# Respacing VectorE's maxima, norms, gates and shifts in the common order of an attention kernel's heads

## The reference

```
q, k, v = x @ Wq, x @ Wk, x @ Wv          # 16 heads of 64
q, k = rmsnorm(q) * wq, rmsnorm(k) * wk
gate = softplus((k . u_n) / 8)            # per key
bias = -max(i - j, 0) * omega_eff * gate[j], -inf above the diagonal
attn = softmax(q @ k.T / 8 + bias);  y = attn @ v
x = layernorm(x + y @ Wproj)
x = layernorm(x + ffn(x))                 # ternary weights, silu * linear, gelu, gelu, linear
```

## Time and profile before

| | us |
|---|---|
| median of 3 runs (3759.3 to 3764.21) | 3760.38 |
| the profiled execution, its own time | 3759.36 |
| its span, first to last instruction | 3757.6 |
| PE busy (matmuls) | 3330.4 |
| VectorE busy | 1934.7 |
| ScalarE busy | 1872.5 |
| GpSimd busy | 1503.4 |
| first and last matmul L835 of the scores | 177.0, 2530.1 |

### The profile page before, as it was taken

One profiled execution on the slowest core, in us unless ns is written; L12 is line 12 of the kernel. 1 busy time (PEld: TensorE's weight loads), 2 busy tenths in 40 slices (PEclk: granted clock), 3 DMA queues, 4 the chain that ended last, 5 costly groups with the idle time before them and its releaser, 6 DMA issues. The chain is left out here.

```text
span 3757.6 us, 46242 instructions
## 1 busy us (share of the span) xinstructions
PE 3330.4 (89%) x16112; PEld 2546.0 (68%) x16112; DVE 1934.7 (51%) x4076; ACT 1872.5 (50%) x3185; POOL 1503.4 (40%) x1304
## 2 busy tenths in 40 slices
PE   2598898898998988989889889896999999899999
PEld 1476675675666766757667667565788877688887
DVE  4566657657657566576565665734322222133232
ACT  0166666666666666666666666673232222232222
POOL 1265565556655655556556555561111111000000
PEclk9999999999999999999999999997999999999999
DMA  1001111011111110111111101105232222221120
GB/s 48 20 24 39 29 32 38 23 32 40 25 42 44 32 37 24 32 39 26 36 28 32 38 24 32 36 24 157 85 99 87 82 84 88 74 96 39 63 68 18
DMA packets 138776, 179.90 MB, mean 48 GB/s; under 512 B 37808, under 2 KB 70192, under 8 KB 138544
## 3 DMA queue, kind: packets, MB, share of 16 engines
q1 hardware_dynamic: 138544, 176.94, 17.1%
HBM read 83.81 MB, written 42.47 MB: 34 GB/s over the span
## 5 line engine op out<-in xcount | busy, mean ns | idle before, releaser
L333 POOL TENSOR_TENSOR e_lo<-e_all,e_hi 128x512 fp32r<-128x512 f32 (+1 forms) x832 | 1042.0, 1257 | 952.7 <-ACT e_all L546 811.9
L546 ACT ACTIVATE e_all<-ps_s,bias 128x512 f32<-128x512 f32 (+3 forms) x1280 | 782.5, 620 | 191.4 <-PE ps_s L838 130.4
L539 ACT ACTIVATE e_hi<-ps_s,bias 128x512 fp32r<-128x512 f32 (+1 forms) x832 | 558.9, 672 | 311.2 <-PE ps_s L836 197.7
L725 DVE TENSOR_REDUCE maxes<-ps_m 128x1 f32<-128x512 f32 x768 | 525.3, 686 | 365.0 <-PE ps_m L811 360.4
L811 PE MATMUL ps_m<-k_ext,q_max 128*128 128x512 f32 (+3 forms) x1280 | 484.9, 392 | 68.2 <-DVE maxes L725 37.8
L835 PE MATMUL ps_s<-q_twice,k_split 128*128 128x512 f32 (+3 forms) x1280 | 492.7, 385 | 0.0
L836 PE MATMUL ps_s<-q_ext,k_ext 128*128 128x512 f32 (+3 forms) x1280 | 479.6, 375 | 0.0
L869 PE MATMUL ps_v<-e_lo,v_main 128*66 128x512 f32 (+1 forms) x832 | 441.0, 530 | 15.7 <-POOL e_lo L333 15.7
L811 PEld LDWEIGHTS ps_m<-k_ext,q_max 128*128 128x128 f32 x1280 | 249.2, 195 | 215.1 <-DVE maxes L725 70.5
L722 DVE CUSTOM_DVE_ANT_0 ps_m<-ps_m,mask_row 128x128 f32<-128x128 f32 (+3 forms) x512 | 252.6, 493 | 247.9 <-PE ps_m L811 244.2
L860 PE MATMUL ps_v<-e_hi,v_rest 128*66 128x512 f32 (+1 forms) x832 | 330.8, 398 | 0.0
(11 more groups left out here) (198 smaller groups left out, 6469.0 us busy)
## 6 DMA issues: line engine op xcount, KB each, us to landing
q_twice<-q_max SPq DMA_DIRECT2D x256, 128.0 KB, 2.3
yt<-y_out SPq DMA_DIRECT2D x128, 130.0 KB
k_split<-k_ext SPq DMA_DIRECT2D x128, 128.0 KB, 2.2
y_in<-yt SPq DMA_DIRECT2D x128, 128.0 KB, 3.1
r_in<-recip_sums SPq DMA_DIRECT2D x128, 128.0 KB, 3.2
hidden<-gelu SPq DMA_DIRECT2D x64, 256.0 KB, 2.0
a_in<-hidden SPq DMA_DIRECT2D x8, 2048.0 KB, 10.9
x_rows<-in_L_attn_x_dram SPq DMA_DIRECT2D x16, 256.0 KB, 3.0
```

Source lines behind the costliest of these rows:

```text
L333: on.tensor_tensor(e_lo[:, i % LO_RING, off:QB], e_all[:, u_ % E_RING, off:QB], e_hi[:, i % HI_RING, off:QB].bitcast(F32), ALU.subtract).t ...
L539: nc.scalar.activation(e_hi[:, i % HI_RING, off:QB], ps_s[u_ % 2][:, off:QB], ACT.Exp, bias=by).then_inc(hi_done, 1)
L546: nc.scalar.activation(e_all[:, u_ % E_RING, off:QB], ps_s[u_ % 2][:, off:QB], ACT.Exp, bias=by).then_inc(ex_done, 1)
L725: nc.vector.tensor_reduce(maxes[:, qt, kc:kc + 1], ps_m[m % 2][:, 0:width], AX.X, ALU.max).then_inc(mx_free, 1)
```

## The change

It gives other due times to some steps. In pair p, with t0 = 2p: "gate a" at t0 - 0.805, "gate exp" at t0 - 0.78, the norms from t0 - 0.80 in steps of 0.035, the parts of "gate b" from t0 - 0.73 in steps of 0.025, the even head's maxima up to t0 + 0.46, the odd head's from t0 + 0.47 to t0 + 1.17, and each shift 0.08 behind the last maximum of its block. No instruction is added or left out, and none computes anything else.

```
-        at(t0 - 0.78, "gate a", p)
-        at(t0 - 0.75, "gate exp", p)
+        at(t0 - 0.805, "gate a", p)
+        at(t0 - 0.78, "gate exp", p)
         for i in range(8):
-            at(t0 - 0.77 + 0.025 * i, "norm", p, i)
+            at(t0 - 0.80 + 0.035 * i, "norm", p, i)
         for i in range(GATE_PARTS):
-            at(t0 - 0.72 + 0.02 * i, "gate b", p, i)
+            at(t0 - 0.73 + 0.025 * i, "gate b", p, i)
...
-            start, end = (turns[1] + 0.03, t0 + 0.28) if s == 0 else (t0 + 0.29, t0 + 1.29)
+            start, end = (turns[1] + 0.03, t0 + 0.46) if s == 0 else (t0 + 0.47, t0 + 1.17)
             for v, (qt, kc) in enumerate(MAXES):
                 qb = qt // TQ
                 when = max(start + (end - start) * v / (NM - 1), turns[2 * qb + 1] + 0.03)
                 at(when, "max", n, v)
                 if v + 1 == maxes_to(qb):
                     at(when + 0.001, "most", n, qb)
-                    at(when + 0.03, "shift", n, qb)
+                    at(when + 0.08, "shift", n, qb)
```

## The result

The changed kernel takes 3774.16 us (median of 7 runs, 3769.09 to 3776.96) against 3760.26 (7 runs, 3756.68 to 3764.21): ratio 1.0034, 95% interval 1.0022 to 1.0046. It is slower by 14 us, where 3743 us, 17 us faster, had been forecast.

The account below looks back on a forecast made before the run. TensorE was taken as the bound, each pair being a 29.8 us VectorE chain plus 120.3 us of TensorE. Terms of -1.0 us a pair, times 15, and -2 once gave 3743 us; range 3717 to 3777.

Parts of the forecast that it names:

- The failed step: In the VectorE chain, the earlier gate Exp holds TensorE and GpSimd some 5 us; TensorE's 10 us to spare make it free.
- the five maxima: They leave the VectorE chain, about -2.9 us of VectorE work, and cost TensorE 1.15 us in the part it bounds.
- Shift 2 behind turn 5: Even head's shift lands right behind an odd head's turn in the same slot: 1.65 us of TensorE waiting.
- First scores of an even head: Their q_twice copies are issued behind shift 1 and come late: +0.35 us a pair, bounds 0 and 1.
- Shift 3's row: Even head's last shift comes close to the scores needing its row: +0.2 us a pair, bounds 0 and 0.5.
- The clock: TensorE's half-speed stretches, about 1.7 us each: one behind shift 0 goes, one behind shift 2 comes; bounds -1.7 and +1.7.
- Before all scores: Once, ahead of attention's first scores, five maxima leave; the q_twice copies then end the wait: -1.5 us.
- The last pair: Final two heads of attention: half of the -1.5 us way back, giving -2 together with the start.
- C: VectorE chain: GpSimd and VectorE exclude each other throughout, all cover comes back, chain 29.7 us, 3785 us; chance 0.09.
- D: Even head: shift 3's row comes too late, a new wait of 0.5 us plus low clock, 3775 us; chance 0.14.
- B: VectorE chain: GpSimd fills half the place of the five maxima, chain only -1.5 us, 3761 us; chance 0.20.
- the signs of being wrong: Chain 29 us or more, gap above 1 us before even heads' scores, odd-head maxima waiting for VectorE, or new low clock.

Follow-up runs that it names:

- Shifts 0.085: The changed kernel with the shifts 0.085 behind their last maximum instead of 0.08: 3767.3 us, ratio 1.0023 to the kernel before.
- values late: Changed kernel with gate Exp at t0 - 0.75, even head's maxima ending at t0 + 0.28, and its GpSimd value copies and splits due later: 3705.2 us.

## Why the prediction was wrong

**The view of the kernel held.** A pair is one VectorE chain and one TensorE part: in all twelve profiles TensorE's first turn follows the end of the last gate link within 0.1 us.

**The failed step** is this one, on what the early Exp holds up: TensorE and GpSimd "stand still meanwhile", "PE has 10 us to spare in this stretch, so that costs nothing". I saw the hold and sized it (5 us; 5.59 measured). I asked whether TensorE had time to spare before its own next wait, and not what else waits for TensorE in that stretch. The emptying does, and it stands in the very queue that bounds. It made VectorE wait 2.4 us a pair, and the chain is 28.95 us where I had forecast 26.9. With the Exp back it is 27.07, and the time is 33 us lower. The mechanism of the five maxima was right in sign and size. I did expect a stretch at low clock in this part of the chain, and called it covered; it falls on the work that the emptying waits for.

**The other terms.** From the turn to the next root the sum was 1.8 us more; measured 1.26. Shift 2 behind turn 5: 1.65 taken, 1.64 measured. First scores of an even head: 0.35 taken, 0.5 measured, for which the profile names no releaser. Shift 3's row: 0.2 taken; no wait in the pair looked at, 0.3 us in the last pair. The clock I took as even, one stretch at half speed going and one coming. One went and none came behind shift 2, but the one behind the turn grew: its two windows of 4 us (0.50 and 0.86, under "Shifts 0.085") lost 2.6 us of TensorE's time, against 1.7 and 1.4 in the two windows of the earlier trace rows. So about 0.6 us was won, and not 0. Before all scores: 1.5 us taken, 1.1 measured (177.0 to 175.9), the wait being for the q_twice copies as forecast.

**The last pair** I covered with half a microsecond. There is no chain there to hide in, TensorE bounds all of it, and it got 3.4 us longer: 1.15 us for the five later maxima, 1.7 us more of waits (3.5 for 1.8), and the rest not followed. With the even head's maxima back it is gone.

**The rivals.** Of C I had written that a chain of 29 us or more would show it. It is 28.95, and C is still wrong: the time was not GpSimd's but a wait. The rule of the Trainium skill ("SBUF — State Buffer", section "Who interferes with whom"), that a VectorE instruction with two inputs in SBUF and a GpSimd one exclude each other, agrees with "values late", where the two-input link L665 takes 1.20 us beside GpSimd's subtractions and 0.23 without them. What I had drawn from it, that GpSimd would take back all that the maxima had covered, the runs don't bear out: without the wait the chain is 2.9 us shorter. D's wait was not there. By my own terms B comes to 3763 and D to 3773 us, and not to 3761 and 3775. No rival had the emptying in it. The measured 3774 us lies inside the range, next to D's time, but that is luck: D is another mechanism, and I had held a faster kernel for the likely outcome. Of the signs of being wrong, the new stretch of low clock did show, in the chain ahead of the emptying; the last gate link's wait is 5.6 us, above the 2 to 5 that I named.

**Open.** Whether VectorE would wait at the emptying if TensorE kept its full clock is not known. Steady pairs take 150.2 us both before and after; the mean difference of 0.3 us comes from early pairs, some of which take 148 us before and 149 to 150 after, and I found no cause for that. Pair 6, where the second sequence's tokens are turned, is 2.8 us longer after the change; a maximum waits 0.9 us there, the rest was not followed.

## What to carry to other kernels

When one engine's chain bounds a stretch, look through that engine's own queue for instructions that wait for the others; slack of another engine is free only up to the first such instruction. A hold is judged by what stands behind it in the held queue, not by its length, and the engine that it stopped may go on at a lower clock (here 0.53 for 5.4 us). And test the parts of a rescheduling alone and in pairs: here each part was the same or faster alone (maxima 5 us, shifts 14.5, gates 4), and together they were 14 us slower.

## What was not expected of the hardware

After standing still for 1.85 and then for 2.79 us TensorE caught up at half its speed: it was busy for 5.40 us on end at a granted clock of 0.53, just when VectorE was about to need its results. By an estimate from that row this is worth as much as the whole wait.

Idleness of TensorE that was removed gave back little. 0.9 us of waits less in a pair made most pairs 0.2 us shorter or less, and TensorE was busy 0.8 us longer with the same 580 instructions. The mean clock of a 4 us window behind the turn was 0.77 for 0.86, which is less than half of it; the rest has no cause that I found.
